# A new table of jobs for a three-layer transformer kernel: k of a batch moves into slots 4 and 6 of the batch ahead of it

## The reference, cut to what matters

```python
x = x + 0.5 * ffn(layernorm(x))          # ffn: fft along 256, a product with a sparse complex w, real(ifft), + bias
x = x + attn(layernorm(x)[..., :128])    # 16 heads of 8, softmax(q k^T / 4) v, then @ Wo.T + bo
x = x + 0.5 * ffn(layernorm(x))
```

## Time and profile before

| | us |
|---|---|
| median of 3 runs | 313.4 (312.87 to 317.94) |
| the profiled execution | 312.38 |
| its span, first to last instruction | 310.5 |
| TensorE busy | 294.8 |
| ScalarE busy | 257.6 |
| VectorE busy | 190.5 |
| GpSimd busy | 98.3 |
| moved by DMA | 49.33 MB |

### The profile page before, as it was taken

The page is one execution under the profiler, slowest core; times in us unless marked ns, Lnnn a source line. Parts: engine busy times, 40 slices in busy tenths (PEclk is TensorE's granted clock), DMA queues, the critical chain, the costliest instruction groups (busy, mean ns, idle before and its releaser), DMA issues.

```text
span 310.5 us, 8810 instructions
## 1 busy us (share of the span) xinstructions
PE 294.8 (95%) x3440; PEld 112.5 (36%) x3443; DVE 190.5 (61%) x552; ACT 257.6 (83%) x285; POOL 98.3 (32%) x113
## 2 busy tenths in 40 slices
PE   8887999899998999999999999999999999998996
PEld 5633333233332333333333333334333333322333
DVE  1688546747775678657776678567755643370255
ACT  2117998898997889998998989998999999999921
POOL 6562531223604053223604251313600340034005
PEclk9999999999999999999999999999999999999999
DMA  7935615573462762665453663554372464112102
GB/s 192 337 137 192 218 65 153 195 270 133 139 217 83 245 208 103 208 204 217 155 192 129 231 205 112 198 172 143 131 238 104 138 205 170 38 68 70 37 34 70
DMA packets 25891, 49.33 MB, mean 159 GB/s; under 512 B 2032, under 2 KB 14192, under 8 KB 24048
## 3 DMA queue, kind: packets, MB, share of 16 engines
q1 hardware_dynamic: 25152, 48.26, 46.0%
q10 hardware_dynamic: 688, 0.40, 0.8%
HBM read 31.08 MB, written 17.56 MB: 157 GB/s over the span
## 4 chain that ended last, share of the span: by engine, by line
PE 75%; DMA 9%; DVE 5%; ACT 5%; issue 3%; POOL 3%; SPq 0%; ACTq 0%; POOLq 0%
PE ot L828 28%; PE misc L719 26%; PE scores L799 15%; ACT probs L669 5%; DMA leftT<-left_scr 4%; DMA q_scr<-qp 2%; PE scores L719 2%; DMA QS<-q_scr 2%; DMA left_scr<-left_blocks 1%; POOL x L553 1%; PE scores L686 1%; PE scores L693 1%; DVE left_blocks L966 1%; DVE lh L957 1%; POOL rstd L550 1%
## 5 line engine op out<-in xcount | busy, mean ns | idle before, releaser
L669 ACT ACTIVATE probs<-scores 128x1024 f32<-128x1024 f32 x256 | 243.8, 1028 | 20.6 <-PE scores L799 20.3
L828 PE MATMUL ot<-probs,VS 128*32 128x512 f32 x1024 | 133.9, 594 | 2.9 <-ACT probs L669 2.3
L799 PE MATMUL scores<-QS,KS 32*128 32x512 f32 x512 | 64.7, 495 | 3.0 <-DMA QS<-q_scr 1.3
L799 PEld LDWEIGHTS scores<-QS,KS 32*128 32x128 f32 x512 | 24.5, 181 | 109.8 <-ACT probs L669 101.0
L828 PEld LDWEIGHTS ot<-probs,VS 128*32 128x32 f32 x1024 | 30.6, 109 | 25.8 <-ACT probs L669 5.0
L563 POOL TENSOR_TENSOR x_out<-x,half_bias 128x512 f32<-128x512 f32 x7 | 9.0, 1292 | 88.8 <-DVE x L1012 88.8
L548 POOL TENSOR_SCALAR veps<-mv 128x4 f32<-128x4 f32 (+1 forms) x25 | 6.1, 242 | 95.9 <-DVE mv L946 95.9
L1017 DVE SCALAR_TENSOR_TENSOR x_out<-misc,rstd,x_out 128x256 f32<-128x256 f32 x28 | 13.5, 484 | 33.7 <-PE misc L719 30.2
L719 PE MATMUL misc<-half_ffn,xT 128*32 128x256 f32 x448 | 32.1, 386 | 0.0
L719 PE MATMUL misc<-half_ffn,xT_in 128*32 128x256 f32 x400 | 27.1, 385 | 1.4 <-DVE half_ffn L1193 1.3
L550 POOL TENSOR_TENSOR rstd<-veps,power 128x4 f32<-128x4 f32 (+1 forms) x25 | 25.3, 1013 | 2.1
(11 more groups left out here) (125 smaller groups left out, 260.0 us busy)
## 6 DMA issues: line engine op xcount, KB each, us to landing
KS<-k_scr SPq DMA_DIRECT2D x14, 512.0 KB, 4.9
QS<-q_scr SPq DMA_DIRECT2D x14, 512.0 KB, 4.6
x_in<-x SPq DMA_DIRECT2D x8, 512.0 KB, 5.1
xT_in<-x_t SPq DMA_DIRECT2D x8, 512.0 KB, 6.4
k_scr<-kp SPq DMA_DIRECT2D x8, 512.0 KB, 3.0
q_scr<-qp SPq DMA_DIRECT2D x8, 512.0 KB, 4.4
x_scr<-x_blocks SPq DMA_DIRECT2D x7, 512.0 KB, 2.9
xT<-x_scr SPq DMA_DIRECT2D x7, 512.0 KB, 4.7
```

The costliest lines, as they stand in the source:

```text
L669: nc.scalar.activation(probs[u % PRING][:, :, :], scores[u % SRING][:, :, :], ACT.Exp, scale=SCORE_SCALE).then_inc(exp_done, 1)
L799: last = mm(scores[(u + j // 2) % SRING][:, j % 2, :], KS[b % 2][rows, slot, kt * P:(kt + 1) * P].bitcast(F32R), QS[b % 2][rows, slot, :]. ...
L828: last = mm(ot[COL * j:COL * (j + 1), :], VS[b % 2][:, kt, h, :], probs[(u + j // 2) % PRING][:, j % 2, :], start=s % 8 == 0, stop=s % 8 == 7)
```

## The change

- `STEADY`: `KT_0`, `KT_1` move from slots 14 and 15 (for two batches ahead) to slots 4 and 6 (one batch ahead); `QT` from 7, 8 to 8, 9; `V_0`, `V_1` from slot 9 to 5 and 7; F1 spreads over slots 0 to 10; `N` from 10 to 11; F2_0 to F2_2 begin one slot later; of F2_3 the first half is now made in slot 15 and the second in slot 0 of the next batch.
- `BEGIN`, `FIRST`, `LATE`, `END` follow; `guard` is in slot 13 for batches 1 to 5 and 12 otherwise.
- SP's order: in a batch, k and q of the next one are stored and loaded after x2 and xT; in the part ahead of the loop q is stored before k is loaded.
- ScalarE's squares, `left_half` and the stats of the first norm move to other slots.

```diff
-STEADY = {0: [("F2_3a", -2, LEFT), ("F2_3", -2, LEFT)], 1: [("F1_0a", 2, LEFT), ("F1_0", 2, LEFT)],
+STEADY = {0: [("F2_3", -2, LEFT), ("F1_0a", 2, RIGHT)], 1: [("F1_0", 2, RIGHT)],
           2: [("WO_0", -1, LEFT), ("WO_1", -1, RIGHT)], 3: [("WO_2", -1, LEFT), ("WO_3", -1, RIGHT)],
-          4: [("F1_1a", 2, LEFT), ("F1_1", 2, LEFT)], 5: [("F1_2a", 2, LEFT), ("F1_2", 2, LEFT)],
-          6: [("F1_3a", 2, LEFT), ("F1_3", 2, LEFT)], 7: [("QT_0", 1, LEFT)], 8: [("QT_1", 1, LEFT)],
-          9: [("V_0", 1, RIGHT), ("V_1", 1, LEFT)], 10: [("N", 1, RIGHT), ("F2_0a", -1, LEFT)], 11: [("F2_0", -1, LEFT)],
-          12: [("F2_1a", -1, LEFT), ("F2_1", -1, LEFT)], 13: [("F2_2a", -1, LEFT), ("F2_2", -1, LEFT)],
-          14: [("KT_0", 2, RIGHT)], 15: [("KT_1", 2, RIGHT)]}
+          4: [("KT_0", 1, RIGHT), ("F1_1a", 2, LEFT)], 5: [("F1_1", 2, LEFT), ("V_0", 1, RIGHT)],
+          6: [("KT_1", 1, RIGHT), ("F1_2a", 2, LEFT)], 7: [("F1_2", 2, LEFT), ("V_1", 1, RIGHT)], 8: [("QT_0", 1, RIGHT)],
+          9: [("QT_1", 1, RIGHT), ("F1_3a", 2, LEFT)], 10: [("F1_3", 2, LEFT)],
+          11: [("N", 1, RIGHT), ("F2_0a", -1, LEFT)], 12: [("F2_0", -1, LEFT), ("F2_1a", -1, RIGHT)], 13: [("F2_1", -1, RIGHT)],
+          14: [("F2_2a", -1, LEFT), ("F2_2", -1, LEFT)], 15: [("F2_3a", -1, LEFT)]}
 
-FIRST = {**STEADY, 0: [("F1_0a", 2, LEFT), ("F1_0", 2, LEFT)], 1: []}
+FIRST = {**STEADY, 0: [("F1_0a", 2, LEFT), ("F1_0", 2, LEFT)], 1: [("F1_1a", 2, LEFT), ("F1_1", 2, LEFT)],
+         4: [("F1_2a", 2, LEFT)], 5: [("F1_2", 2, LEFT), ("V_0", 1, RIGHT)], 6: [("QT_0", 1, RIGHT)], 7: [("QT_1", 1, RIGHT)],
+         8: [("F1_3a", 2, LEFT)], 9: [("F1_3", 2, LEFT)], 10: [("V_1", 1, RIGHT)]}
 
 BEGIN = {3: [("LT", 1, LEFT)], 4: [("KT_0", 1, RIGHT), ("F1_0a", 2, LEFT)], 5: [("F1_0", 2, LEFT), ("QT_0", 1, RIGHT)],
          6: [("KT_1", 1, RIGHT), ("F1_1a", 2, LEFT)], 7: [("F1_1", 2, LEFT), ("QT_1", 1, RIGHT)],
-         8: [("F1_2a", 2, LEFT), ("F1_2", 2, LEFT)], 9: [("F1_3a", 2, LEFT), ("F1_3", 2, LEFT)],
-         10: [("V_0", 1, RIGHT), ("V_1", 1, LEFT)], 11: [("N", 1, RIGHT)], 12: [("LT", 2, LEFT)],
-         13: [("KT_0", 2, RIGHT)], 14: [("KT_1", 2, LEFT)]}
-
-LATE = {0: [("F2_3a", -2, LEFT), ("F2_3", -2, LEFT)],
+         8: [("F1_2a", 2, LEFT), ("F1_2", 2, LEFT)], 9: [("V_0", 1, RIGHT), ("F1_3a", 2, LEFT)],
+         10: [("F1_3", 2, LEFT), ("N", 1, RIGHT)], 11: [("V_1", 1, RIGHT)],
+         13: [("LT", 2, LEFT)], 14: [("KT_0", 2, RIGHT)], 15: [("KT_1", 2, RIGHT)]}
+
+LATE = {0: [("F2_3", -2, LEFT)],
         2: [("WO_0", -1, LEFT), ("WO_1", -1, RIGHT)], 3: [("WO_2", -1, LEFT), ("WO_3", -1, RIGHT)],
-        5: [("QT_0", 1, LEFT)], 6: [("QT_1", 1, LEFT)], 7: [("V_0", 1, RIGHT)], 8: [("V_1", 1, LEFT)],
-        9: [("F2_0a", -1, LEFT)], 10: [("F2_0", -1, LEFT), ("N", 1, RIGHT)], 11: [("F2_1a", -1, LEFT)], 12: [("F2_1", -1, LEFT)],
-        13: [("F2_2a", -1, LEFT)], 14: [("F2_2", -1, LEFT)]}
-END = {0: [("F2_3a", -2, LEFT), ("F2_3", -2, LEFT)],
+        4: [("KT_0", 1, RIGHT)], 5: [("KT_1", 1, RIGHT)], 6: [("QT_0", 1, RIGHT)], 7: [("QT_1", 1, RIGHT)],
+        8: [("V_0", 1, RIGHT)], 9: [("V_1", 1, RIGHT), ("F2_0a", -1, LEFT)], 10: [("F2_0", -1, LEFT), ("N", 1, RIGHT)],
+        11: [("F2_1a", -1, LEFT)], 12: [("F2_1", -1, LEFT)],
+        13: [("F2_2a", -1, LEFT)], 14: [("F2_2", -1, LEFT)], 15: [("F2_3a", -1, LEFT)]}
+END = {0: [("F2_3", -2, LEFT)],
...
-    return 12 if it else 13
+    return 13 if 0 < it < B - 2 else 12
...
             k_out(1)
+            q_out(1)
             k_in(1)
-            q_out(1)
             q_in(1)
             for it in range(1, B):
-                if it + 1 < B:
-                    k_out(it + 1)
                 if it >= 2:
                     store_out(it - 2, 1)
                 if it + 3 < B:
                     load_x(it + 3)
-                if it + 1 < B:
-                    k_in(it + 1, slice(0, 1))
                 x2_through(it - 1)
-                if it + 1 < B:
-                    k_in(it + 1, slice(1, None))
                 xT_in_from(it - 1)
                 if it + 1 < B:
+                    k_out(it + 1)
+                    k_in(it + 1)
                     q_out(it + 1)
+                    q_in(it + 1)
                 if it + 2 < B:
                     left_through(it + 2)
-                if it + 1 < B:
-                    q_in(it + 1)
+                store_out(it - 1, 0)
                 if it + 2 < B:
                     leftT_in(it + 2)
-                store_out(it - 1, 0)
...
-                    if s == (2 * 4 if it else 2 * 8):
+                    if s == (2 * 7 if it == B - 2 else 2 * 8):
                         square(kp, sq_k, kp_step, it + 1)
-                    if s == (2 * (8 if it == B - 2 else 10) if it else 2 * 9):
+                    if s == (2 * 11 if 1 < it < B - 2 else 2 * 9):
                         square(qp, sq_q, qp_step, it + 1)
...
-                        if s == (8 if it else 10):
+                        if s == 12:
                             left_half(it + 2, range(0, 2))
-                        if s == (9 if it else 10):
+                        if s == (13 if it else 12):
                             left_half(it + 2, range(2, T))
                             if it:
                                 turn_left(it + 2)
                     if it + 3 < B:
-                        if s == 11:
+                        if s == 6:
                             norm0_stats(it + 3, range(0, 2))
-                        if s == 13:
+                        if s == 8:
                             norm0_stats(it + 3, range(2, T))
                             norm_moments(0, it + 4)
```

## The result

| | before | after |
|---|---|---|
| median of 6 runs each | 312.56 (310.87 to 317.94) | 318.79 (316.25 to 321.63) |
| ratio, 95% interval | | 1.018 (1.011 to 1.025) |
| profiled execution; its span | 312.38; 310.5 | 316.25; 314.5 |

The changed kernel is slower by about 1.8%. 318.8 us is inside the range of 310 to 319, at its upper end, and 4.8 us above the 314.0 that was forecast. Medians are of all executions of a kernel; ratios and their intervals leave out those more than 1.5% above its fastest. Note that the profiled execution of the changed kernel is the fastest of its six: the profile explains 4.0 of the 6.2 us between the medians, and the rest has to be found in others.

The account below looks back on a forecast made before the run. TensorE, busy 95% of the span, was taken as the bound. Batch 0 -0.6, batch 1 -1.2, batches 2 to 5 +1.2, batch 6 +1.9, batch 7 -0.2 gave +1.1; forecast 314.0 us, range 310.0 to 319.0.

Parts of the forecast that it names:

- the slot model: TensorE, steady batches: double slots 2.29 us, single 1.86; ten and six as before, sum 34.1, gain 0.
- take_values: Slot 8, batches 2 to 5: values wait for VectorE to free `ot`, about 0.3 each, +1.1 us for four.
- the wait for left_half: Batch 0, slot 13: LT waits because F1_3 of batch 2 is now in slot 10; +0.8 us, up to +1.3.
- The order of SP's queue: Batches 1 and 6: k's store behind x2 and xT makes a 25.1 us chain, QS late by 1.05 and 1.7.
- batch 1: Whole batch: -0.7 us for slots, -1.5 for the leftT wait, +1.05 for late QS; together -1.2.
- GpSimd's next_x keeps its distance: GpSimd's next_x, from slot 11 and wanted in slot 1: priced at nothing, one slot of 1.9 us if it fails once.
- N costs the same wherever it stands: Steady table: moving N to another slot changes no cost; slot sum stays 34.1 us, gain 0.
- a GpSimd or VectorE chain holds a slot in each batch: Rival: moved norm stats and left_half hold a slot per batch, 4 x 1 us more, 318; chance 0.07.
- the wait at the end of batch 6: End of batch 6: 25.1 us transfer chain against 23.4 of slots, QS late by +1.7 us, 0 to 2.5.
- The steady QS: Batches 2 to 5: QS chain of 10.0 us fits 10.2 of slots; booked 0.1 a batch, +0.4, ends 0 and 1.9.
- Rows in time everywhere: Rival: fast stores and loads remove the QS lateness of 1.05, 1.7 and 0.4; about 311 us, chance 0.28.
- QS late at every boundary: Rival: slow q store and load make QS 2.0 us late in each of batches 2 to 5; about 321, chance 0.10.

Follow-up runs that it names:

- experiment 6: Changed kernel with take_values ahead of the norm's stats in slot 7: median 318.10 us, ratio 1.019 to the kernel before.
- experiment 2: Changed kernel with GpSimd's x_in bias passes moved ahead of the power for left_half: median 317.56 us, ratio 1.014 to the kernel before.
- experiment 4: Changed kernel with q stored before KS is loaded in batch 6 alone: median 315.5 us, ratio 1.011 to the kernel before.
- experiment 7: Changed kernel with GpSimd's passes earlier, q stored before KS loads in batches 1 and 6, take_values first in slot 7: median 312.46 us, ratio 0.999 to before.
- experiment 8: Kernel of experiment 7 with, in batch 0, F1_3 whole in slot 9, V_0 in 10, left_half in 11: 311.90 us, ratio 0.997 to before.
- experiment 9: Kernel of experiment 8 with KT_1, QT earlier, V later in steady batches, q stored before KS everywhere, squares earlier: 310.46 us, ratio 0.992 to before.
- experiment 5: Changed kernel with 16 small products of zeros on TensorE at the head of batch 6's slot 15: median 318.23 us, ratio 1.018 to before.
- run 1: Changed kernel again, unaltered, as base for others: median 318.81 us, ratio 1.017 to the kernel before.
- experiment 3: Changed kernel with q stored before KS is loaded in batches 1 and 6 alone: median 315.13 us, ratio 1.012 to the kernel before.

## Why the prediction was right, and where it was off

**Right, with its size.** This is the slot model: ten double and six single slots, no gain from the table itself. Batch 5, the one steady batch with only the forecast costs, took 34.53 against a forecast of 34.4 + 0.3. *take_values*: slot 8 at 2.16 for 1.91, 0.25 a batch for 0.3 forecast, shown by experiment 6. Batch 0 changed by -0.45 for -0.6, with the wait for left_half at 0.92 (0.8 forecast). The order of SP's queue made QS late before batches 2 and 7 and nowhere else in the first profile. Batch 6 grew by 2.17 for 1.9, of which 1.5 (1.7 forecast) are the wait and 0.65 (0.2 forecast) other slots.

**Right in sign, not in size: batch 1.** QS was late by only 0.26 for the 1.05 forecast, but the transfers were no quicker: from the start of slot 3 (70.14) to the scores (95.98) the chain took 25.8 for the 25.1 forecast, its q store 7.1 (83.64 to 90.78) for 6.4. The slots it had to fit into were longer too, 25.6 for 24.0. Slots 7, 8 and 13 are together 1.4 us longer than three single slots, which the forecast had not counted. Slot 13 is GpSimd's passes (0.6, gone in experiment 2). In slots 7 and 8 ScalarE's two squares fall next to each other (78.98 and 81.31); that they cause the 0.7 there is argued and not shown, but experiment 6 leaves both slots as they were, so it is not take_values.

**The step that failed** is the sentence that GpSimd's next_x keeps its distance and is priced at nothing. Its distance to who needs its result was kept; what was not asked is beside whom it runs. Before, the passes waited for the first norm's stats in slot 13 and ran from slot 15 on, beside the splits of k, which read `misc` in PSUM and at most one SBUF tensor:

```profile
165.85 1.28 POOL L563 TENSOR_TENSOR x_in<-x_in,half_bias 128x512 f32<-128x512 f32 x1
```

The splits at 165.52, 166.94 and 167.40 took 0.42 each beside them. In the changed kernel those stats are made by slot 8, and GpSimd's program has the passes right behind the power for left_half, which waits for the stats of F1_3 in slot 10: so the passes fall on left_half and on `on`. That is 2.5 us in batches 2 to 4 and another 0.6 in batch 1, and experiment 2 shows both. With batch 1 the sentence that N costs the same wherever it stands fails too. It belongs to the rival "a GpSimd or VectorE chain holds a slot in each batch", 4 x 1, which was given 0.07.

**The term that was mis-sized** is the wait at the end of batch 6. It was priced at its own length, 1.7 us with an end of 2.5. In the first profile it cost about that, 1.5. In the second it was 2.3, and the clock fell behind it: slots 15 and 0 cost 1.5 us more, in experiment 2 even 2.7 more. Removing that wait was worth 3.3 us by the medians (experiment 4), double its forecast. It is also where the two profiles of the changed kernel differ: their spans by 2.3 us (314.5 and 316.8), batches 6 and 7 together by 2.3.

**The range held in part by luck.** 318.8 is 0.2 under its high end, and three of the six executions lie above it. The sum was +1.1 and the medians differ by 6.2. The high end of 319.0 was worked out from QS 2.0 late in batch 1, 2.5 in batch 6 and 0.8 in every steady batch; the first profile has 0.26, 1.5 and none. What filled the range instead is GpSimd's 3.1 us, priced at nothing, and the clock behind the wait of batch 6, which the forecast doesn't mention.

**The steady QS** was booked at 0.4 and cost nothing in the first profile, but only since slots 8 and 14 were already longer. As soon as those costs were taken away, it appeared: 0.1 to 1.0 in experiments 2, 6, 7 and 8. "It fits by 0.2" was a fair reading: in batch 3 of the first profile q was stored from 155.74 and QS asked for at 160.41, 4.67 for the 4.6 forecast.

**The rivals.** "Rows in time everywhere" was worked out at 311. Experiment 9 has all rows in time and measured 310.5, but that is no test of the 311: it also takes away the costs of take_values and of left_half in batch 0, 1.1 and 0.8, which the rival kept. "QS late at every boundary" did not come.

What remains open: experiment 5's median, which should have been lower by about 1 us, and what makes the 0.7 us of batch 1's slots 7 and 8.

## What to carry to other kernels

When work moves to another slot, check not only when its result is wanted but which instruction of a neighbouring engine it will now run beside: here GpSimd's passes beside `on`, `left_half` and `norm_max` cost VectorE up to 1.9 us at a time, and moving the passes made them meet `norm_max` of another batch. Price a wait of TensorE by what follows it too: in three profiles here its clock was lower behind such a wait. And where a transfer chain fits its deadline by tenths, what is won upstream can come back as a wait there, as in experiments 2, 6, 7 and 8: relax the deadline first, then remove the costs; in experiment 9 the spread fell to 1.4 us once that was done.

## What the runs showed of the hardware that was not expected

- GpSimd's x_in passes stretched VectorE's `on` from 0.42 to 0.85 us and a pair of `left_half` from 0.60 to 1.56, and the second of them was stretched itself from 1.28 to 1.48. Two operations on 16 numbers each (`norm_max`), 0.36 together elsewhere, took 2.27 beside them: what they lost was not limited by their own length.
- TensorE busy for 0.77, 0.30 and 0.28 of 3 us (experiments 1, 2 and 6) was followed by a granted clock of 0.57, 0.50 and 0.78 over the next 3; busy for 1.53 of 3, or with filler products for all 3, by 1.00. Eight value products took 1.96 us at the lower level and 1.04 at the upper.
- The order of the queue alone moved the load of QS in batch 6 from 264.40 to 258.94. A q store issued right behind two KS loads took 6.4 us to land there, 6.1 in run 1 and 7.1 in batch 1; one ahead of them took 4.7 at most in batch 6 and 3.1 at most in batch 1 of experiment 3.
